# Two-layer transformer on one core: the FFN's output opens the sum's bank, second layer's transposes ahead of the output projection, low part of attention ahead of the row maximum

## What is computed

```python
xn = layernorm(x)                                    # first layer
q, k, v = (xn @ w + b for w, b in ...)               # 16 heads of 128
a = softmax(q k^T / sqrt(128) - 1e10 * (1 - mask))   # causal
x = x + (a v) @ w_o + b_o + ffn0(xn)                 # ffn0: fp8 operands, gelu(gate) * ff1, bf16 result
xn = layernorm(x)                                    # second layer
q, k, v = ...                                        # 16 heads of 16, no mask
x = x + (softmax(q k^T / 16) v) @ Wo + bo + ffn1(xn) # ffn1: silu(gate) * up, with Hadamard transforms
```

## Time and profile before

| | us |
|---|---|
| median of 3 runs | 980.52 |
| lowest and highest | 976.35, 980.92 |
| the profiled execution's own time | 982.77 |
| its span, first to last instruction | 980.7 |

### The profile page before, as it was taken

The page is one execution under the profiler, slowest core; times in us unless marked ns, Lnnn a source line. Parts: engine busy times, 40 slices in busy tenths (PEclk is TensorE's granted clock), DMA queues, the critical chain, the costliest instruction groups (busy, mean ns, idle before and its releaser), DMA issues.

```text
span 980.7 us, 22791 instructions
## 1 busy us (share of the span) xinstructions
PE 900.6 (92%) x7965; PEld 723.5 (74%) x8032; DVE 755.2 (77%) x2128; ACT 680.5 (69%) x1997; POOL 348.4 (36%) x637
## 2 busy tenths in 40 slices
PE   4877889899999999999999999999999999987797
PEld 2434667677788878888888888888888888866575
DVE  6787676667878887888788888888878887877576
ACT  4787687457767777777767776777677767776464
POOL 5502357334333333333333333333323333333243
PEclk9878999999999999999999999999999999999799
DMA  9242360002000200020002000100011000100000
GB/s 306 85 149 62 123 204 13 1 3 81 1 1 11 63 11 14 2 70 3 23 2 63 10 23 2 51 22 23 1 35 38 23 1 12 50 1 23 1 13 11
DMA packets 46879, 39.96 MB, mean 41 GB/s; under 512 B 4400, under 2 KB 42032, under 8 KB 46512
## 3 DMA queue, kind: packets, MB, share of 16 engines
q1 hardware_dynamic: 46768, 38.52, 12.8%
HBM read 30.11 MB, written 8.39 MB: 39 GB/s over the span
## 4 chain that ended last, share of the span: by engine, by line
PE 60%; DVE 17%; ACT 10%; issue 5%; POOL 0%; another core or an unknown queue 0%; ACTq 0%; DVEq 0%; POOLq 0%
PE ps L823 32%; PE ps L949 6%; ACT arena L1172 5%; DVE arena L816 5%; PE ps L872 4%; DVE arena L817 4%; PE ps L1048 3%; PE ps L1066 3%; ACT arena L812 3%; PE ps L845 3%; DVE arena L1332 3%; PE ps L1077 2%; PE ps L907 2%; PE ps L1050 1%; ACT arena L811 1%
## 5 line engine op out<-in xcount | busy, mean ns | idle before, releaser
L817 DVE SCALAR_TENSOR_TENSOR arena<-ps,bqk,arena 128x256 bf16<-128x256 f32 x416 | 187.5, 479 | 76.3 <-ACT arena L812 76.3
L812 ACT ACTIVATE arena<-ps,bqk 128x256 bf16<-128x256 f32 x416 | 177.9, 463 | 80.8 <-PE ps L1050 62.7
L816 DVE TENSOR_TENSOR arena<-ps,arena 128x512 bf16<-128x512 f32 (+1 forms) x336 | 204.1, 633 | 23.6 <-ACT arena L811 23.2
L823 PE MATMUL ps<-arena,wqkv 128*128 128x256 bf16 x1728 | 217.0, 277 | 2.5 <-DVE arena L816 2.5
L811 ACT ACTIVATE arena<-ps 128x512 bf16<-128x512 f32 (+1 forms) x336 | 180.8, 558 | 35.8 <-PE ps L872 21.4
L1563 POOL TENSOR_SCALAR arena<-arena,rc 128x128 f32<-128x128 f32 (+1 forms) x256 | 106.3, 429 | 272.6 <-DVE rc L1361 272.5
L1172 ACT ACTIVATE arena<-arena,nb 128x128 f32<-128x128 f32 (+1 forms) x256 | 114.4, 447 | 126.9 <-DVE nb L1332 126.8
L1570 POOL TENSOR_SCALAR arena<-arena,rc 128x256 f32<-128x256 f32 x254 | 119.0, 482 | 221.7 <-DVE rc L1365 221.7
L823 PEld LDWEIGHTS ps<-arena,wqkv 128*128 128x128 bf16 x1728 | 171.6, 99 | 26.9 <-issue 1.7
L1172 ACT ACTIVATE arena<-ps,nb 128x256 f32<-128x256 f32 x256 | 119.3, 478 | 20.3 <-DVE nb L1339 20.2
L823 PE MATMUL ps<-arena 128*128 128x128 bf16 (+2 forms) x864 | 98.9, 251 | 13.5 <-DVE arena L817 6.5
(11 more groups left out here) (115 smaller groups left out, 1278.5 us busy)
## 6 DMA issues: line engine op xcount, KB each, us to landing
scratch_qk<-arena SPq DMA_DIRECT2D x28, 128.0 KB, 1.9
arena<-scratch_qk SPq DMA_DIRECT2D x84, 32.0 KB, 1.8
arena<-scratch_qk SPq DMA_DIRECT2D x42, 64.0 KB, 2.5
arena<-in_x SPq DMA_DIRECT2D x4, 512.0 KB, 9.4
arena<-in_w_gating SPq DMA_DIRECT2D x4, 512.0 KB, 8.3
arena<-in_w_q SPq DMA_DIRECT2D x4, 512.0 KB, 4.6
arena<-in_w_k SPq DMA_DIRECT2D x4, 512.0 KB, 5.6
arena<-in_w_v SPq DMA_DIRECT2D x2, 1024.0 KB, 6.6
```

Source lines behind the costliest of these rows:

```text
L812: return nc.scalar.activation(out, in_, ACT.Identity, bias=bias)
L816: return nc.vector.tensor_tensor(out, in_, hi, ALU.subtract)
L817: return nc.vector.scalar_tensor_tensor(out=out, in0=in_, scalar=bias, in1=hi, op0=ALU.add, op1=ALU.subtract)
L823: last = nc.tensor.matmul(out, lhsT, rhs, start=(n == 0), stop=(n == len(steps) - 1))
```

## The change

Five things:

1. **Bank opening.** `open_bank` of the first layer goes. At a sequence's first head (`h == 0`) one matmul of `identb` and the whole `ybin` (512 columns) opens `BK_X` in place of the ones and the bias; the two matmuls at the last head go. `open_y` remains for the second layer's bank, and `brow` holds `bo` alone.
2. **Bias `b_o`.** GpSimd adds it to the residual rows (`bias_rows0`, two adds of 128x256 f32 a sequence, in the step with `s % 16 == 1`, after that step's `norm_0` and `norm_1`); `x1_sum` waits for `rows_biased` in place of `rows_ready`. The splitting and copying of `b_o` at the opening goes.
3. **y's load** is issued in step 1 for the first sequence and in step 10 of each sequence for the next one.
4. **TensorE, ScalarE, VectorE:** `turn1` goes ahead of `project_out0`; `p1_high` ahead of `p0_high`; `p1_low` ahead of `p0_low`.
5. **VectorE:** `o0_low` goes ahead of `max_0`.

```diff
         ones = sb("ones", [P, P], BF16)
-        brow = sb("brow", [P, 2, 512], BF16)
+        brow = sb("brow", [P, 512], BF16)
         st = sb("st", [P, B * TT, 6], F32)
...
 
-        bo = sp0[:, 0:2, 0:D]
-        bo_hi = pt0[:, :, 0, 0:D]
-        bo_rest = bias_room[:, 0:2 * D].rearrange("p (w d) -> p w d", w=2)
-        bo_mid = oT0[:, 0, :, :]
+        bo = sp0[:, 0, 0:D]
+        bo_hi = pt0[:, 0, 0, 0:D]
+        bo_rest = bias_room[:, D:2 * D]
+        bo_mid = oT0[:, 0, 0, :]
+        bo_rows = bias_room[:, 0:D]
 
...
             load_x(3)
-            for w, name in enumerate(("bo0", "bo1")):
-                sp.dma_start(bo[:, w, :], t[name].partition_broadcast(P)).then_inc(biases_loaded, 16)
+            for place, name in ((bo_rows, "bo0"), (bo, "bo1")):
+                sp.dma_start(place, t[name].partition_broadcast(P)).then_inc(biases_loaded, 16)
             sp.dma_start(mask[:, :], t["mask"]).then_inc(consts_loaded, 16)
...
             nc.gpsimd.memset(ones[:, :], 1.0)
-            nc.gpsimd.memset(brow[:, :, :], 0.0).then_inc(half_ready, 1)
+            nc.gpsimd.memset(brow[:, :], 0.0).then_inc(half_ready, 1)
             pool.wait_ge(half_ready, 2)
...
                 for i in range(2):
-                    last = nc.vector.tensor_copy(brow[r:r + 1, :, i * D:(i + 1) * D], part[r:r + 1])
+                    last = nc.vector.tensor_copy(brow[r:r + 1, i * D:(i + 1) * D], part[r:r + 1])
             last.then_inc(bias_rows, 1)
...
 
-        rows_ready = [sem(f"rows_ready{i}") for i in range(2)]
+        rows_ready, rows_biased = [sem(f"rows_ready{i}") for i in range(2)], sem("rows_biased")
         spilled = [[sem(f"spilled_{w}{i}") for i in range(2)] for w in "qk"]
...
 
-            def open_bank(bank, closing=False):
-                nc.tensor.matmul(ps[:, bank, :], ones[:, :], brow[:, int(bank != BK_X or closing), :], start=True,
-                                 stop=False)
+            def open_y(bank):
+                nc.tensor.matmul(ps[:, bank, :], ones[:, :], brow[:, :], start=True, stop=False)
 
...
                     weights_ready(pe, ("wo0", h // 8))
-                if n == 0:
-                    pe.wait_ge(bias_rows, 1)
                 if h == 0:
-                    upto(pe, x1_done, b)
-                    open_bank(BK_X)
-                if h == H0 - 1:
                     if b == 0:
...
                     pe.wait_ge(y_ready, 16 * (b + 1))
-                    for i in range(TT):
-                        nc.tensor.matmul(ps[:, BK_X, i * D:(i + 1) * D], identb[:, :], ybin[:, i, :], start=False,
-                                         stop=False)
+                    upto(pe, x1_done, b)
+                    nc.tensor.matmul(ps[:, BK_X, :], identb[:, :], ybin[:, :, :].rearrange("p i d -> p (i d)"),
+                                     start=True, stop=False)
                 pe.wait_ge(o0_lo, n + 1)
...
                     pe.wait_ge(p1_lo, 1 + max(m for m in range(B * H1) if turn1_bank(m) == BK_X))
+                if n == 0:
+                    pe.wait_ge(bias_rows, 1)
                 if k == 0:
-                    open_bank(y_bank(b), True)
+                    open_y(y_bank(b))
                 pe.wait_ge(h1_lo, n + 1)
...
                     turn0(s - 2)
-                if 0 <= s - 4 < NG0:
-                    project_out0(s - 4)
                 for n in heads_in[s - 1]:
...
                         turn1(n)
+                if 0 <= s - 4 < NG0:
+                    project_out0(s - 4)
                 if v_in(s) is not None:
...
                     qk0_high(s)
+                for n in heads_in[s - 1]:
+                    if not second(n):
+                        p1_high(n)
                 if 0 <= s - 2 < NG0:
...
                     split_high(act, c, 0)
-                for n in heads_in[s - 1]:
-                    if not second(n):
-                        p1_high(n)
                 for n in heads_in[s]:
...
                 dve.wait_ge(out0_ps, H0 * (b + 1))
-                dve.wait_ge(rows_ready[b % 2], 16 * (b // 2 + 1))
+                dve.wait_ge(rows_biased, b + 1)
                 nc.vector.tensor_tensor(rows[:, b % 2], ps[:, BK_X, :].rearrange("p (i d) -> p i d", i=TT), rows[:, b % 2],
...
                             mask_q()
-                if 0 <= s - 1 < NG0:
-                    max_0(s - 1)
                 if 0 <= s - 4 < NG0:
                     o0_low(s - 4)
+                if 0 <= s - 1 < NG0:
+                    max_0(s - 1)
                 if last:
...
                     qk0_low(s)
-                if 0 <= s - 2 < NG0:
-                    p0_low(s - 2)
                 for n in heads_in[s - 1]:
...
                         p1_low(n)
+                if 0 <= s - 2 < NG0:
+                    p0_low(s - 2)
                 fold(s)
...
 
+            def bias_rows0(b):
+
+                if b == 0:
+                    pool.wait_ge(biases_loaded, 32)
+                pool.wait_ge(rows_ready[b % 2], 16 * (b // 2 + 1))
+                for i in range(TT):
+                    v = rows[:, b % 2, i, :]
+                    last = nc.gpsimd.tensor_tensor(v, v, bo_rows, ALU.add)
+                last.then_inc(rows_biased, 1)
+
             def rstd_1(b):
...
                     split_low_pool(pool, c, 1)
+                if s % H0 == 1 and s > H0:
+                    bias_rows0(s // H0 - 1)
                 if s == split_slot[("dn", 0)] - 1:
...
             def load_y(b):
-                if b == 0:
-                    sp.wait_ge(y_stored, 16 * PAIRS)
-                upto(sp, out0_ps, H0 * b)
+                sp.wait_ge(y_stored, 16 * (b // 2 + 1))
+                if b:
+                    sp.wait_ge(out0_ps, H0 * (b - 1) + 1)
                 sp.dma_start(ybin[:, :, :], y_d[TT * b:TT * b + TT].rearrange("i p d -> p i d")
...
                     sp_later_y(sp, PAIRS - 1)
-                if g == 10 and b < B:
-                    load_y(b)
+                if s == 1:
+                    load_y(0)
+                if g == 10 and b + 1 < B:
+                    load_y(b + 1)
                 if s == 8:
```

More of the change, by code:

```diff
@@ L1480, in dve_program @@
                             mask_q()
+                if 0 <= s - 4 < NG0:
+                    o0_low(s - 4)
                 if 0 <= s - 1 < NG0:
                     max_0(s - 1)
-                if 0 <= s - 4 < NG0:
-                    o0_low(s - 4)
                 if last:
```

## The result

The changed kernel takes 991.17 us (median of 4 runs, 989.45 to 992.17), the kernel before, run beside it, 980.72. The ratio is 1.0109, with a 95% interval of 1.0087 to 1.0130: slower by about 1.1%, which is more than the 0.5% that a measurement of this kernel can tell from no change. The profiled execution took 991.44 us, its span is 989.5. One execution of all that are told of here, of the kernel with the copies behind the maximum, took 2346.7 us where its other four took 964.97 to 966.26, and stands in no ratio.

A forecast was written before the change was run, and what follows sets the result against it. TensorE, busy 92% of 980.7 us, bounds the kernel, with a chain across engines bounding some steps. Terms −2.2 + 5.7 + 0.9 + 5.6 + 0.2 = +10.2 against the median of 980.5 gave 990.7 us, range 979 to 998.

The forecast's parts named there:

- The middle terms: Filling, 97 to 241: +5.7 us; steps 241 to 365: +0.9; steady batches from 365 to 859: +5.6.
- The two outer ones: Terms at both ends of the span: opening −2.2 us, end from 859 +0.2 us.
- The loop and the fourth swap: Maximum's end to next step: 4.35 to 3.89 us; o0_low ahead of the maximum pays back 0.40, leaving 0.05.
- A steady batch: One batch of 16 steps from 467.6: +1.13 us; 4.75 such batches from 365 to 859 give +5.6.
- Steps 241 to 365: Steps behind the filling: the first ones +0.4, the rest like half a batch; together +0.9 us.
- The filling: 97 to 241, no second layer yet: o0_low delays the maximum; +5.7 us, including −0.2 for y; bounds 0 to +6.5.
- Rival 2: Filling steps absorb their delays: +1.5 there, +6 in all, 986.5 us (983.5 with half the steady loss); chance 0.18.
- The opening: Bias-row copies 0.6 earlier, VectorE's L260 starts ahead of GpSimd's L267; −2.2 us, bounds −0.4 and −2.5.
- The end: From 859: turn1's transposes 0.6 earlier at 894 and 901, two late maxima cost 0.4 each; +0.2 us, bounds −2 and +2.
- Rival 1: Bound steps: maximum delayed under 0.1 instead of 0.40, swaps keep their gain; −13, 967.5 us; chance 0.12.
- Rival 3: GpSimd's new adds hold VectorE's cast L1417, 0.7 in 8 batches; +5.6 more, 996.3 us; chance 0.15.
- The signs named: turn0 waits above 12 us, attend0's ≤ third, batch 103.3, quiet maximum 1.74, scores0 waiting for p0_low, L260 at 84.6.

The follow-up runs named there:

- the copies behind the maximum: Changed kernel with max_0 ahead of o0_low again, and the six bias-row copies moved behind the first max_0: 965.87 us, 0.9822 of the kernel before.
- the maximum first: Changed kernel with only max_0 put ahead of o0_low again: 964.91 us, 0.9814 of the kernel before; measured again, 966.38 us.
- the low part first alone: Kernel before with only o0_low put ahead of max_0: 1006.42 us, ratio 1.0236.
- the bank alone: Kernel before with the new bank opening, GpSimd's bias adds and y's load, all four orders as before: 975.16 us, ratio 0.9916.
- the swaps alone: Kernel before with turn1, p1_high and p1_low first, o0_low and bank as before: 968.97 us, ratio 0.9855.
- the maximum first in the filling only: Changed kernel with max_0 ahead of o0_low in the first 28 steps only: 985.53 us, 1.0050 of the kernel before.
- high and low parts swapped but TensorE not: Kernel before with p1_high ahead of p0_high and p1_low ahead of p0_low, TensorE's order unchanged: 984.65 us, ratio 1.0030.
- the last two experiments: Changed kernel with max_0 first, once with bias-row copies moved behind the first max_0 (965.87 us), once without that move, measured again (966.38 us).

## Why the prediction was right, and by which steps

The forecast was 990.7 us (979 to 998), slower with a chance of 0.74; measured were 991.2. The middle terms were right in size and place. The two outer ones were both missed, by −5.1 and +3.1 us, and that they cancel in the main is luck; so is that the total fell within 0.5 us: the two profiled executions lie 8.7 us apart, the medians 10.4, where the sum had 10.2.

- **The loop and the fourth swap** (4.35 to 3.89, then 0.40 back): right. The kernels with the maximum first show the loop's gain whole, the steady batch at 100.4, and those with the low part first show it paid back: +2.9 a batch with the swaps, +2.9 without. The bound step of the earlier trace rows takes 5.92 us before, 5.46 with the maximum first, 5.85 in the changed kernel (−0.07; predicted −0.06) and 6.32 with the low part first alone.
- **A steady batch** +1.13: measured +1.07 (by the starts of the steps). By steps: the one from 467.6 +0.48 (predicted +0.51), 486.9 and 493.0 together +0.22 (+0.27), 499.9 +0.21 (+0.18), 527.2 +0.10 (0), 533.5 +0.11 (+0.23), and 546.1, 557.9 and 564.0 each within 0.02. The sum to 859 was +5.45 for 5.6 (which is more than 4.75 times 1.13, 5.4: the prediction doesn't show how it counts the part batch). The stall in the step from 493 was 1.00, or 1.17 with the modelled end, for 1.21.
- **Steps 241 to 365** +0.9: measured +1.28.
- **The filling** +5.7: measured +6.05, in the steps named (224.4: +1.01 for +1.0), and worth 5.6 by the run that undid it alone. The −0.2 for y at 187.6 did not come (0.00). Rival 2 (it absorbs them) is out.
- **The opening** −2.2: the mechanism and its size were right, the term as a whole was not, since something was left out. The copies gave −0.54 (predicted −0.6), and from the first step to the second the trace shows −1.84, which is L260 and its maximum: −2.4 together. The rest of the −7.3 by the fifth step, 4.9 us, is what the term put at nothing, and most of it goes with TensorE's clock. 2.2 of it lie ahead of the first step, at a granted clock of 0.91 from 0 to 80 in place of 0.87, and 2.8 between the second step and the fifth. TensorE in the kernel before stood 4.8 us ahead of the second step and was granted 1.2 GHz for long pieces of 85 to 110 (a mean of 0.80); in the changed kernel it stood 3.0 and kept 2.4 GHz. But the shorter idle is not enough to keep the clock: with the maximum first (both traces), in the bank alone and with the filling's order undone TensorE stands the same 3.0 us there, and is granted 0.86. These four traces need 18.5 to 18.7 us from the second step to the fifth, where the kernel before needs 19.3 and the changed one 16.5. So 0.6 to 0.9 of the 2.8 go with the new opening. Up to the fourth step the changed kernel gives TensorE, ScalarE and VectorE the same order as they do, and takes 10.31 us from the second to there where they take 11.43 to 11.45; that 1.1 us is chance of its profiled execution. What keeps the clock stays open.
- **The end** +0.2: measured +3.3, and as much against the kernel with the maximum first. The `turn1` gain of 0.6 did not come in the sum (with the swaps alone the part from the last steady step on is 0.1 shorter than before). The first four steps take 1.9 more than with the maximum first, where 0.8 was predicted for two late ones. The two stretches of the changed kernel, from the last steady step on:
```profile
858.21:890.97 32.76, 27.27 (x252) 21.80 (x250) 23.42 (x67) 22.48 (x73) 11.14 (x25) 0.95 0.01 2
890.97:989.50 98.53, 80.43 (x705) 60.10 (x702) 64.39 (x151) 51.45 (x161) 33.13 (x66) 0.93 0.04 12
```
The same two in the kernel with the maximum first:
```profile
834.89:865.78 30.89, 25.74 (x252) 20.83 (x250) 23.28 (x67) 22.69 (x73) 11.15 (x24) 1.00 0.01 2
865.78:962.90 97.12, 79.35 (x705) 59.35 (x702) 64.07 (x151) 51.24 (x161) 33.08 (x65) 0.95 0.04 12
```
TensorE's work is the same, at a lower clock: of the 1.87 more in the first stretch its busy time holds 1.53, of the 1.41 in the second 1.08. How much is the late maximum's own shows where the clock is the same. With the maximum first in the filling only, it is late here and TensorE keeps its full clock:
```profile
852.78:884.87 32.09, 25.84 (x252) 20.81 (x249) 23.26 (x67) 22.46 (x73) 11.15 (x25) 1.00 0.01 2
```
That is 1.2 us more than the 30.89 at the same clock, so the late maxima cost 1.2 and not 0.8, and the other 0.7 goes with the lower clock. The second stretch takes 98.5 to 99.3 us at 0.93 in three kernels: the changed one, the one with the maximum first in the filling only, and the one with high and low parts swapped but TensorE not, whose maximum stands first. With the low part first alone it takes less than in the kernel before (96.3 at 0.95):
```profile
908.29:1004.00 95.71, 78.68 (x707) 59.30 (x704) 63.87 (x151) 51.63 (x161) 31.90 (x64) 0.96 0.04 12
```
So, as far as one profile of each can tell, the late maximum is neither needed for the lower clock nor enough for it; what brings it on stays open.
- **Rival 1** (the maximum is not delayed where it counts) gave 967.5 as its time, and the kernel in which it isn't delayed took 964.9. Its condition failed: `o0_high` is not there before the scores.
- **Rival 3** (GpSimd's adds hold VectorE's cast): the mechanism is real, the price was not. The one cast of 0.97 in the earlier trace rows ran beside GpSimd's L1592 (from 230.05). In the bank alone the cast takes 0.85 in place of 0.29 once for each of seven sequences, with the adds (L1582) beside it:
```profile
574.86 1.46 POOL L1582 TENSOR_TENSOR arena<-arena 128x256 f32<-128x256 f32 x2
...
574.88 0.85 DVE L1414 CAST arena<-arena 128x256 bf16<-128x256 f32 x1
```
The maximum behind it starts at 575.76, where the scores are there at 575.73, so nothing waits; the step is the 6.54 us that it was. With the maximum first it is the same seven times (0.70 to 0.72, once 0.84), and the batch is as long as with the swaps alone (100.39 and 100.42). In the changed kernel the adds do so once only, at 905.87.
- **The signs named**: `turn0`'s waits well above 12 (19.9), the batch at 103.3 (103.29) and the quiet step's 1.74 (1.78) came true. `attend0`'s wait at a third or less did not (4.8 of 7.6): the late maximum arrives there too. The new wait of `scores0` for the low part of p0 did not come: there are 9 such waits before and after (9.0 and 10.1 us), all while filling. L261 took the 1.2 us named, but at 82.44 and not 84.6.

## What to carry to other kernels

Before a ready piece of work is put ahead of the head of the chain, ask what it waits for itself: here `o0_low` fits into no gap, since its input comes as late as the scores, and 0.40 us of it, paid once a step by an engine that is idle a quarter of the time, cost 26 us (23 without the other edits). Swaps along a chain belong together: halves of this one gave −3.6 and +3.7 us, the whole 14.5. And where a forecast is a sum of terms with both signs, look at the terms again even if the total is right: here the ends were off by 5.1 and 3.1 us, with opposite signs.

## What the runs showed of the hardware

- VectorE's and GpSimd's operations on SBUF held each other in several pairs: the subtraction of 128x1024 takes 1.22 us when it is first, 2.67 and 3.07 when it starts 0.54 and 0.13 behind GpSimd's; GpSimd's, when second, 2.81 in place of 2.12. Unexpected was that operations with one input are held as well: the cast of 128x256 (0.85 for 0.29), and even copies of a single row of 256 (2.09 for 0.71, four of them). Not every pair does so: VectorE's scaling L1441 of 128x256 f32 at 500.16 in the kernel before takes its usual 0.40 us, though it starts 0.17 before the end of GpSimd's L1570. The Trainium skill, SBUF — State Buffer, section "SBUF: two separate sides", describes such a lock, for VectorE's operations with two SBUF inputs or in a mode that uses two ports. The subtractions agree with it; which mode the casts, the copies and the scaling run in, no run here shows.
- In the opening, what goes with TensorE's granted clock (most of 4.9 us) is more than what the order of that lock gives (1.84). The clock differs between executions of one kernel: the first step started at 80.45 us in one profile, with a mean of 0.94 ahead of it, and at 81.56 in the other, with 0.91. In the nine executions of the kernel before beside the last two experiments the time goes with the mean clock: 985.5 and 986.1 us at 0.974, 981.5 to 981.8 at 0.981.
